# Attention and mixture-of-experts layer: expert rows in two groups of batches and 128-row units instead of three groups and 256-row pairs, with sums begun level by level

## What is computed

```python
x = L0_attn_x                                   # 16 batches, T = 512 tokens, C = 256
x = layernorm(x + attention(x, wq, bq, ...))    # 16 heads of 16, rotary, causal
# feed-forward, for each token:
probs = softmax(x @ gate_w.T)                   # 32 experts
top_w, top_idx = top_k(probs, 8)
top_w = top_w / sum(top_w)
for each expert e (guw, dw):
    g, u = split(x @ guw.T)
    y = u * silu(g) @ dw.T
    acc = acc + y * w_e                         # w_e is 0 outside the top 8
x = layernorm(x + acc)
```

## Time and profile before

| what | value |
|---|---|
| median of 3 runs | 2143.23 us (2139.93 to 2151.34) |
| the profiled execution, its own time | 2155.9 us |
| span of its trace | 2154.1 us |
| busy: TensorE, VectorE, ScalarE, POOL | 83%, 74%, 62%, 57% |
| mean granted TensorE clock | 0.944 |

### The profile page before, as it was taken

How to read it: one execution, slowest core, us unless ns; L and a number is a source line. 1 busy time by engine, 2 the same in 40 slices (tenths; PEclk the granted TensorE clock), 3 DMA queues, 4 the chain that set the end, 5 groups by cost and what they waited for, 6 DMA issues and landing times. The chain is left out here.

```text
span 2154.1 us, 53487 instructions
## 1 busy us (share of the span) xinstructions
PE 1789.0 (83%) x16894; PEld 1265.4 (59%) x16894; DVE 1595.9 (74%) x3572; ACT 1339.6 (62%) x3228; POOL 1223.1 (57%) x1190
## 2 busy tenths in 40 slices
PE   4899888898988888898878979998888889898920
PEld 2455554455544454455446868887777777787820
DVE  4788788888888778887854545565456777778988
ACT  1566665656644654555447868887767677798820
POOL 1003456444653465444544777777777777777760
PEclk8999999999999999999888999999999999999965
DMA  4355677667765766556566756656689899889977
GB/s 139 113 163 180 204 229 241 201 206 228 242 205 164 261 218 219 188 179 209 197 225 220 261 181 209 210 194 190 209 303 302 296 303 319 294 287 349 364 243 249
DMA packets 240425, 495.01 MB, mean 230 GB/s; under 512 B 47928, under 2 KB 135391, under 8 KB 230384
## 3 DMA queue, kind: packets, MB, share of 16 engines
q1 hardware_dynamic: 162400, 307.69, 46.2%
q0 software_dynamic: 56064, 155.31, 19.4%
q10 hardware_dynamic: 21696, 28.58, 3.9%
HBM read 284.54 MB, written 234.04 MB: 241 GB/s over the span
## 5 line engine op out<-in xcount | busy, mean ns | idle before, releaser
L1268 ACT ACTIVATE pT<-ps 128x512 f32<-128x512 f32 (+2 forms) x1008 | 663.8, 700 | 302.5 <-PE ps L1050 249.4
L880 POOL DMA_INDIRECT x_sorted<-xhl,idx x512 | 520.8, 1017 | 469.0 <-DVE xhl L1692 232.3
L1617 DVE TENSOR_REDUCE mn<-ps 128x1 f32<-128x512 f32 (+3 forms) x704 | 413.4, 633 | 54.4 <-PE ps L1024 51.7
L1116 PE MATMUL ps<-pT,gu_hi 128*128 128x256 f16 (+1 forms) x1600 | 372.0, 250 | 52.1 <-ACT pT L1268 51.7
L1117 PE MATMUL ps<-pT,gu_hi 128*128 128x256 f16 (+1 forms) x1600 | 370.7, 250 | 0.0
L1118 PE MATMUL ps<-pT,gu_lo 128*128 128x256 f16 (+1 forms) x1600 | 370.3, 249 | 0.0
L898 POOL DMA_INDIRECT y_tokens<-work,yidx x264 | 279.9, 1060 | 79.8 <-issue 60.3
L1022 PE MATMUL ps<-stacks 96*128 96x512 bf16 (+3 forms) x1024 | 275.4, 313 | 49.2 <-DMA stacks<-qk_parts 20.2
L1048 PE MATMUL ps<-stacks 99*128 99x512 bf16 (+3 forms) x1024 | 285.7, 309 | 26.1 <-ACT pT L1268 20.6
L1050 PE MATMUL ps<-maskk,identb 128*128 128x128 bf16 x1024 | 223.3, 223 | 0.0
L1116 PEld LDWEIGHTS ps<-pT,gu_hi 128*128 x1600 | 157.9, 99 | 78.4 <-issue 64.4
(11 more groups left out here) (238 smaller groups left out, 3756.4 us busy)
## 6 DMA issues: line engine op xcount, KB each, us to landing
stacks<-y_tokens SPq DMA_DIRECT2D x64, 1024.0 KB
stacks<-qk_parts SPq DMA_DIRECT2D x128, 192.0 KB
qk_parts<-pbuf SPq DMA_DIRECT2D x31, 768.0 KB, 4.2
stacks<-qk_parts SPq DMA_DIRECT2D x128, 128.0 KB
attention<-yev ACTq DMA_DIRECT2D x64, 256.0 KB
stacks<-x_sorted SPq DMA_DIRECT2D x52, 304.0 KB, 4.3
x_sorted<-pads_h SPq DMA_DIRECT2D x99, 152.0 KB
pbuf<-x_sorted SPq DMA_DIRECT2D x40, 304.0 KB
```

The costliest lines, as they stand in the source:

```text
L880: pool.indirect_dma_start(xsort[g][:, :], bass.IndirectOffsetOnAxis(ap=at, axis=0), xhl_rows[:, t, :], None).then_inc(s_scat, 16)
L1116: mmul(o, w_hi[k], x_hi[k], start=k == 0, stop=False)
L1268: return nc.scalar.activation(o, i, f, **k)
L1617: V.tensor_reduce(mn[:, tt, h0:h0 + nh], ps[:, odd_bank("max", at, m), 0:nh * n].rearrange("p (a n) -> p a n", a=nh), axis=AX.X, op=ALU.ma ...
```

## The change

The batches form two groups, 12 and 4. All blocks are two 128-row units, each with its own entry of the table, so that `NPAIR`, `NSINGLE`, the pieces and the three-row table go. In a group the units are ordered by **level** (four batches, in the last group two): first the units of every expert with rows of the first level, then those of the next. The number of slots becomes 104 + 40, `S = 144`. The sums of a level stand in the order from 9 slots after the slot that ends the level, a tile in 1.6 slots while there are slots, so the first at slot 49. One DRAM array takes the rows of all tokens. A sorted row is 1280 bytes, was 1216, since the destination is now a float beside the weight; ScalarE copies both at once and makes the four indices of a slot whole in a fifth copy. The table is computed by a shorter program, for the first group in the last iteration of the first part, for the second in slots 23 to 27. The work of batch 15 stands in 23 slots, and its scatters from slot 24, one in two slots. Batch 14's scatters stand in slots 0 to 14.

```diff
-GROUPS = ((0, 7), (7, 13), (13, 16))
+GROUPS = ((0, 12), (12, 16))
+LEVELS = ((0, 4), (4, 8), (8, 12), (12, 14), (14, 16))
...
-NPAIR = [(hi - lo) * T * TOPK // BLK - E // 2 for lo, hi in GROUPS]
-NSINGLE = 2 * E
-NSLOT = [n // 2 + NSINGLE // 4 for n in NPAIR]
-SLOT0 = [sum(NSLOT[:g]) for g in range(NG + 1)]
+NTAB = [(hi - lo) * T * TOPK // UNIT + E for lo, hi in GROUPS]
+TAB0 = [sum(NTAB[:g]) for g in range(NG + 1)]
...
+SLOT0 = [n // 4 for n in TAB0]
 S = SLOT0[-1]
...
-RW = 2 * C + 3 * E
+RW = 2 * C + 4 * E
...
+    for l, (lo, hi) in enumerate(LEVELS):
+        at = max(at, 10 * (LEVEL_END[l] + FIRST_TILE))
         for q in range(lo * NT, hi * NT):
+            pace = 16 if at < 10 * S else 10
...
-    early = [(B - 2, j) for j in range(NT * TOPK) if (j // 6 if j < 12 else 2 + (j - 12) * 34 // 20) == k]
-    return early + [(B - 1, j) for j in range(NT * TOPK) if LATE_SCATTER + j * 3 // 2 == k]
...
+    early = [(B - 2, j) for j in range(NT * TOPK) if (j // 6 if j < 12 else 2 + (j - 12) * 13 // 20) == k]
+    return early + [(B - 1, j) for j in range(NT * TOPK) if LATE_SCATTER + 2 * j == k]
...
+LATE_SCATTER = 24
+LATE_TABLE, LATE_TABLE_OUT, LATE_TAILS = 23, 30, 32
...
-                if pieces(n) == 1:
-                    src = xsort[g][bass.ds(x_row(n, 0), BLK), :].rearrange("(p m) c -> p m c", m=2)
-                    sp.dma_start(xrows[HOMES[n]], src).then_inc(s_xs[HOMES[n]], 16)
-                    return
                 for m in range(2):
                     sp.dma_start(xrows[HOMES[n]][:, m, :], xsort[g][bass.ds(x_row(n, m), UNIT), :]).then_inc(s_xs[HOMES[n]], 16)
...
-                if first == 0:
+                if q == LEVELS[l][0] * NT:
                     for k in range(NYR):
-                        wait(sp, s_ys[k], stored(last_of(k, 2 * SLOT0[g + 1])))
+                        wait(sp, s_ys[k], stored(last_of(k, 2 * LEVEL_END[l])))
...
+                for n in (2 * s, 2 * s + 1):
+                    for m in range(2):
+                        c = 2 * (n % NIDX) + m
+                        actv(yrow[:, c, :].rearrange("p (o k) -> p o k", o=1),
+                             xpair[HOMES[n]][:, m, bass.ds(expert(n, m), 1), :], ACT.Copy).then_inc(s_iy, 1)
+
+            def whole_indices(s):
+
+                wait(act, s_iy, copied(2 * s))
+                c = 4 * s % (2 * NIDX)
+                actv(yidx[:, c:c + 4], yrow[:, c:c + 4, 1], ACT.Copy).then_inc(s_iy, 1)
...
-                    if i > 1:
-                        end_of_routing(i, e)
+                    if i == NB - 1 and e >= SLOT_TABLE:
+                        unit_table(0, e - SLOT_TABLE)
```

More of the change, by code:

```diff
@@ L159 @@
 LOADS_AT = loads_plan()
[L160 to L180, removed]
@@ L183, in table_columns @@
[L183 to L194, removed]
+EARLY_HOMES, LATE_HOMES = list(range(12)), list(range(12, 18)) + list(range(8, 12))
+LATER = (2 * LEVEL_END[0] - 20) // 12 * 12
@@ L197, in stored, with copied @@
+HOMES = [EARLY_HOMES[n % 12] if n < LATER else LATE_HOMES[(n - LATER) % 10] for n in range(2 * S)]
+NXR = 18
 def stored(n):
     return 32 * (n // NYR + 1)
+def copied(n):
+    return 5 * (n // 2 + 1) - 1
 def indexed(n):
-    return 2 * sum(pieces(k) for k in range(n + 1))
+    return copied(n) + 1
 def scatters_at(k):
-    early = [(B - 2, j) for j in range(NT * TOPK) if (j // 6 if j < 12 else 2 + (j - 12) * 34 // 20) == k]
-    return early + [(B - 1, j) for j in range(NT * TOPK) if LATE_SCATTER + j * 3 // 2 == k]
@@ L213 @@
[L213 to L219, removed]
+    early = [(B - 2, j) for j in range(NT * TOPK) if (j // 6 if j < 12 else 2 + (j - 12) * 13 // 20) == k]
+    return early + [(B - 1, j) for j in range(NT * TOPK) if LATE_SCATTER + 2 * j == k]
+LATE_SCATTER = 24
+LATE_TABLE, LATE_TABLE_OUT, LATE_TAILS = 23, 30, 32
+LATE = {"residual": 0, "den": 1, "num": 2, "recip": 3, "rec_out": 4, "rec_in": 5, "divide": 7, "project": (9, 10), "add": (9, 10),
+        "stats": (10, 11), "rsqrt": 12, "mean": 13, "norm": 14, "store": 16, "x1": (16, 17), "x1_out": (16, 17), "split": 17,
+        "lower": 18, "router": 19, "router_in": 19, "choice": (19, 20), "mask": 20, "exp": 21, "rank": 22, "rank_in": 22,
+        "weights": 22}
@@ L222, in last_of, with slots @@
+def slots(i):
+    return LATE if i >= B else EACH
 def last_of(r, end):
@@ L232, in loaded @@
 def loaded(n):
[L234 to L241, removed]
-def table_of(i):
-    return [g for g, (lo, hi) in enumerate(GROUPS) if hi == i]
+    return 32 * len(uses_before(n) + [n])
+GROUP_OF = [g for g in range(NG) for _ in range(NTAB[g] // 4)]
 def y_bank(n):
@@ L252, in y_on_vector @@
 def y_on_vector(n):
[L253 removed]
+    return n % 2 == 1
 def max_group(i, e):
@@ L300, in odd_plan @@
                         take(i, "fin", p - 2)
-                if place == 0 and e == SLOT_TABLE_OUT and table_of(i - 1):
-                    take(i, "table", i - 1)
+                if place == 0 and (i, e) in TABLE_OUT:
+                    take(i, "table", TABLE_OUT.index((i, e)))
                 if place == 1:
@@ L1105, in table_transpose @@
                 wait(pe, s_tcomp, TB[g + 1])
-                k = odd.take(s_tab, g + 1, "table", GROUPS[g][1])
-                for part, at in enumerate((0, NPAIR[g])):
-                    last = nc.tensor.transpose(ps[0:3, k, at:at + P], tcol[part][:, 0:3], ident[:, :])
+                k = odd.take(s_tab, g + 1, "table", g)
+                for n in range(NLANE[g]):
+                    last = nc.tensor.transpose(ps[0:2, k, n * P:(n + 1) * P], lanes[:, n, :], ident[:, :])
                 last.then_inc(s_ttr, 1)
@@ L1455, in _ @@
                         max_out(max_group(i, e))
-                    if e in SLOT_X1_OUT and end:
-                        x1_out(i - 1, SLOT_X1_OUT.index(e))
+                    if e in slots(i)["x1_out"] and end:
+                        x1_out(i - 1, slots(i)["x1_out"].index(e))
                     if e in SLOT_VALUES and nxt:
@@ L1492, in _ @@
                     rows_copy(2 * (k - LAG) + 1)
-                if k == LATE_SPLIT:
+                if i == NB and e == slots(i)["split"]:
                     upper_rows(NB - 1)
-                if e == SLOT_EXP and i == NB:
+                if i == NB and e == slots(i)["exp"]:
                     router_exp(i - 1)
@@ L1515, in _ @@
             V.tensor_copy(base[:, :], base0[0]).then_inc(s_set, 1)
+            for first in IN_GROUP:
+                V.memset(level[:, (first[0] + IN_GROUP.index(first)) * E:(first[0] + IN_GROUP.index(first) + 1) * E], 0.0).then_inc(s_set, 1)
             for kc in range(NC):
```

407 lines of the change are left out of this document (196 added, 211 removed).

## The result

| | time, median us (runs) | range of runs | profiled execution, own time | its span |
|---|---|---|---|---|
| before | 2146.53 (8) | 2139.93 to 2156.12 | 2155.9 | 2154.1 |
| after | 2123.86 (8) | 2117.68 to 2128.09 | 2119.02 | 2116.0 |

The ratio is 0.9878, with a 95% interval of 0.9857 to 0.9898: faster by 1.2%, some 26 us, where 69 were forecast; 2123.86 us lies above the range's upper end of 2112. What follows compares spans, and so must explain why they fell by 38 and not by 69.

The account below looks back on a forecast made before the run. The prediction took POOL, full with indirect DMAs and their gaps, to bound the second part. Its terms, -39 (blocks and sums), -13 (attention) and -17 (end), made -69 us, from 2143.2 to 2074 us, range 2048 to 2112.

Parts of the forecast that it names:

- Fewer blocks: Second part: 152 slots become 144, 32 fewer `y_tokens` DMAs on POOL at 1.28 us each, -41 us.
- more sums: Second part: 56 sums instead of 51 begin while POOL works, at 0.46 us each, +2 us.
- Single units on TensorE: Block slots: all-single slots take TensorE 4.88 us, below POOL's 5.1 and more, so no cost.
- ScalarE and VectorE: Block slots: 4.9 us on ScalarE and 5.7 on VectorE against POOL's 5.8, no cost, up to 20 us in the range.
- Batch 15's chain: Early slots, with batch 14's scatters: waits lie behind POOL's backlog, 0 us; one slot's 5 us if that cover goes.
- SP, 0: SP's queue in the second part: 576 load issues instead of 400 and more waits for stored rows, 0 us, bound +6.
- Tables and tails: Attention part: table work leaves iterations 8 and 14, a shorter one enters 15, one tail-fill run leaves; -13 us, between -4 and -18.
- The end: After POOL's last DMA: the last level has 8 tiles instead of twelve, 4 x 4.25 us, -17 us.
- Weight loads set TensorE's pace: Rival, block slots: products and turns come 78 ns apart, 6.3 us a slot, 2104 us; chance 0.03.
- The crowded loop: Rival, second part: the 85 slots with sums take 6.3 us rather than 5.8, +42, 2116 us; chance 0.17.
- The transfers saturate: Slower rival, 85 slots with sums: stored rows land late and POOL idles; at 275 GB/s +102, 2176 us; chance 0.08.
- Only the blocks count: Rival: slots go, but iteration 15's table and the last level's load waits cancel the other gains, 2104 us; chance 0.09.

Follow-up runs that it names:

- static_gu: Changed kernel with gate and up weights from a fixed expert, so TensorE computes no address for them (wrong output); ratio to before 0.9695.
- static_pe: Changed kernel with fixed experts for gate, up and down and no table reads on TensorE, so no register instructions in its blocks; ratio to before 0.9730.
- share: Changed kernel with the second unit of a block reusing the first's gate and up weight address, products and loads unchanged; ratio to before 0.9704.
- wide: Changed kernel with both units of a block on the first's gate and up expert, in products of 256 columns; ratio to before 0.9643.
- levels_off: Changed kernel with one level for each group, so a group's sums begin only when all its blocks are stored; 2238.55 us, ratio to before 1.0404.
- before_split: Kernel before, with a pair's gate and up products issued as two of 128 columns sharing one computed address; ratio to before 0.9991.

## Why the prediction was wrong

**Fewer blocks, -41, and more sums, +2: the size was right, but nothing guaranteed that POOL stays the bound.** With the addresses gone (static_gu, static_pe) or halved (share, wide), POOL's section is 883.3, 882.4, 882.8 and 885.5 us; forecast was 885. In the change it is 913.5.

**"Single units on TensorE ... Cost nothing, hidden by POOL" is the step that failed.** It cost 30 us (913.5 - 883). Two things were wrong in it. The 2.44 us came from one single slot between pairs. There the sequencer had run ahead: in the slots of pairs it has 16 register instructions fewer to do, so ready instructions pile up, which one single slot can use. A kernel of single units has no such slot. (That the store is filled in the pairs is read from rows 6 and from the fifteen quick products above; no run filled or emptied it by itself. That the addresses cost the 30 us is shown.) And the term counted products only, not the 1.92 us of register instructions and table reads a slot, whose rows, at before's 1.24 us a slot, stood in the trace of before. The prediction counted what SP's and POOL's queues have to do, not what TensorE's has. The missing 29 us of POOL's section (913.5 against 885) are nearly all of the 31 by which the spans fell short of the forecast.

**ScalarE and VectorE, 0:** right in the main; levels_off bounds it at 6.5 us. **Batch 15's chain, 0:** right, POOL is not idle over 0.33 us before 1285 us. **SP, 0:** right; with the same 576 loads static_gu keeps POOL full.

**Tables and tails, -13:** 14.4 in this pair of profiles. Over four traces with the attention part of before (start at 1164.6 to 1171.6) and ten with that of after (1143.4 to 1159.5) the means are 1167.9 and 1151.4 us, 16.5 apart: inside the bounds.

**The end, -17:** 13.5. The 4.25 us a tile held, but the first tile of the last level waits 6.21 us for its load of `y_tokens`, where before an output was waited for 3.48 us. 52.3 us, forecast 49.

**The rivals.** "Weight loads set TensorE's pace" (0.03, 2104 us) named the engine and nearly the time of a slot (6.3 us), though 78 ns a product was too much for the mean of 66.0, and it named it as a property of weight loads, which before_split excludes. It was set aside because of rows 6, the very rows that misled the sum. The crowded loop got 0.17 and has at most 6.5 us. The list of what would show it did hold the right sign, products more than 60 ns apart; but one has to take their mean. The Trainium skill's 81 ns (TensorE: Matmul & The Clock Gate, "Back-to-back issue gap") stand near the 80 of the drained stretch in after, where register instructions stand between the products, and do not agree with share (58.2) and before_split (59.1), in which every product has its load too. "The transfers saturate" did not happen: from 1300 to 2020 us static_gu moves 301 GB/s, after 290, and static_gu's POOL is full. "Only the blocks count" is out as well: the start came 14.4 us sooner and the end was 13.5 us shorter, and the blocks are what fell short.

Where the range failed: it ended at 2112, and took TensorE above POOL for nearly excluded. The upper bound of the term should have been the sequencer's whole work added to the 4.88 us, 6.8 us a slot and hence no gain from the blocks.

Three of the prediction's sums do not come out. The bounds of its terms add to -29 (-39 + 20 + 5 + 6 - 4 - 17) and -74 (-39 - 18 - 17), not to -36 and -82; an upper end of 2114 us would have failed too. In TensorE's pace, 144 slots of 6.29 us are 906 us, not 900, so its price was 2110 us. Five sums more at 1.9 us are 9.5 us, not 8; nothing rested on that.

## What to carry to other kernels

When a bound is lowered, every engine close behind it needs its own count, and the count must take in what its sequencer does (register arithmetic, table reads), which busy time leaves out. A pace read from one stretch holds only if that stretch repeats; after a stretch of long instructions a queue may have a store that flatters the next. An address that two products share is worked out once; where a change halves the products' width and gives each its own, cost the addresses and not the products, and move multiplications out to where the value is loaded.

## What was not expected of the hardware

- Register instructions on TensorE's sequencer lasted 46 ns (multiply and add, 37 with a scaled value) and 32 ns (addition), and were hidden in the kernel before, at 1.24 us a slot, with products of 256 columns and with 128 (before_split).
- Reading table entries into registers took about 80 ns an entry: 676 ns for 8, 1318 ns for 16. Larger reads saved nothing in the reading itself.
- In ten traces with the attention part of after (four of them with other levels or more entries a read) its end lay between 1143.4 and 1159.5 us. A pair of profiles can thus differ by 16 us in a stretch that no edit touched; POOL's section, where POOL was full, agreed within some 3 us in four kernels (882.4 to 885.5) and within 2 in the four of before (922.3 to 924.2), and is the better thing to compare.
